# One kernel of four layers on Trainium2: the last score waves of the first attention in bank pairs, with one exponential for two heads

## The reference, cut to what matters

```python
h = layernorm(layernorm(x))                       # gamma, beta
q, k, v = heads(h @ w_qkv + b_qkv)                # 16 heads of 8 channels
scores = q @ k.T / sqrt(8)                        # 1024 x 1024 for each head
out = softmax(scores) @ v
x = x + x_in_norm + out @ w_out + b_out           # residuals
```

## Time and profile before

| | |
|---|---|
| median of 3 runs | 2932.99 us (2932.86 to 2940.77) |
| the profiled execution's own time | 2927.33 us |
| its span, first to last instruction | 2925.5 us |
| mean granted TensorE clock | 0.985 |
| first and last exponential of the first attention (L780) start | 68.1 and 860.1 us |
| busy in the span: PE, DVE, ACT, POOL | 94%, 79%, 72%, 62% |

### The profile page before, as it was taken

The page is one execution under the profiler, slowest core; times in us unless marked ns, Lnnn a source line. Parts: engine busy times, 40 slices in busy tenths (PEclk is TensorE's granted clock), DMA queues, the critical chain, the costliest instruction groups (busy, mean ns, idle before and its releaser), DMA issues.

```text
span 2925.5 us, 46589 instructions
## 1 busy us (share of the span) xinstructions
PE 2744.2 (94%) x16447; PEld 2037.2 (70%) x16447; DVE 2307.5 (79%) x4143; ACT 2100.6 (72%) x4692; POOL 1802.3 (62%) x1357
## 2 busy tenths in 40 slices
PE   6999999999899999999999999999999999999996
PEld 3333333333347777788888888888888888888885
DVE  8888888888937887778788777788777877777776
ACT  2777777777755555677777777777777777787773
POOL 3432534332115555677788778788778787777873
PEclk9999999999979999999999999999999999999997
DMA  1000000000021121000000000000000000000000
GB/s 41 7 7 7 12 7 7 7 7 2 2 76 53 47 73 59 8 1 1 1 1 3 1 3 3 3 1 3 3 1 3 3 1 3 3 1 3 3 3 6
DMA packets 25689, 34.83 MB, mean 12 GB/s; under 512 B 4136, under 2 KB 14952, under 8 KB 25456
## 3 DMA queue, kind: packets, MB, share of 16 engines
q1 hardware_dynamic: 25456, 31.85, 3.5%
HBM read 29.08 MB, written 2.23 MB: 11 GB/s over the span
## 4 chain that ended last, share of the span: by engine, by line
PE 69%; DVE 10%; ACT 10%; POOL 5%; issue 5%; DMA 0%; DVEq 0%; POOLq 0%
PE P L1792 17%; PE P L1817 11%; PE P L1660 9%; PE P L1645 5%; PE P L1721 5%; PE P L1803 5%; PE P L1633 4%; ACT a_PT L780 4%; PE P L1826 3%; PE P L1732 3%; PE P L1775 2%; PE P L1623 2%; DVE c_nm L1371 2%; ACT c_P L904 2%; POOL d_tn L1094 2%
## 5 line engine op out<-in xcount | busy, mean ns | idle before, releaser
L1371 DVE TENSOR_REDUCE c_nm<-P 128x1 f32<-128x1024 f32 x512 | 623.8, 1218 | 169.3 <-PE P L1792 169.1
L1216 DVE TENSOR_REDUCE a_mx<-P 128x1 f32<-128x512 f32 x1024 | 640.1, 683 | 94.9 <-PE P L1633 91.6
L904 ACT ACTIVATE c_P<-P,c_nm 128x1024 f32<-128x1024 f32 x512 | 576.0, 1125 | 131.6 <-DVE c_nm L1371 131.4
L780 ACT ACTIVATE a_PT<-P 128x512 f32<-128x512 f32 x1024 | 537.2, 602 | 165.5 <-PE P L1645 165.1
L2039 POOL TENSOR_TENSOR c_P<-c_P,c_P 128x1024 f32<-128x1024 f32 (+1 forms) x256 | 623.2, 2434 | 21.4
L2037 POOL TENSOR_SCALAR c_P<-c_P,c_rr 128x1024 f32<-128x1024 f32 (+1 forms) x256 | 304.4, 1189 | 305.0 <-DVE c_rr L1383 304.9
L1792 PE MATMUL P<-c_xth,c_Th 128*128 128x512 f32 x1024 | 365.8, 438 | 42.8 <-ACT c_P L904 42.6
L1645 PE MATMUL P<-a_Qs,a_Ks 32*128 32x512 f32 x1024 | 343.0, 491 | 59.1 <-ACT a_PT L780 52.6
L1817 PE MATMUL P<-c_DT,c_xkh 128*128 128x256 f32 x2048 | 392.0, 284 | 5.6 <-DVE c_xkl L1363 5.0
L1396 DVE TENSOR_TENSOR c_DT<-P,c_DT 128x512 fp32r<-128x512 f32 x512 | 348.6, 681 | 12.9 <-ACT c_DT L915 12.1
L1817 PEld LDWEIGHTS P<-c_DT,c_xkh 128*128 128x128 f32 x2048 | 330.1, 192 | 6.6 <-DVE c_xkl L1363 5.6
(11 more groups left out here) (245 smaller groups left out, 5418.4 us busy)
## 6 DMA issues: line engine op xcount, KB each, us to landing
b_cwB<-cw_scratch SPq DMA_DIRECT2D x64, 256.0 KB, 5.1
c_stg<-in_cw SPq DMA_DIRECT2D x8, 640.0 KB, 3.9
a_Qs<-a_mT SPq DMA_DIRECT2D x256, 2.0 KB
b_stg<-in_moe SPq DMA_DIRECT2D x9, 384.0 KB, 3.1
out<-xres SPq DMA_DIRECT2D x15, 128.0 KB, 1.8
xres<-in_x SPq DMA_DIRECT2D x3, 512.0 KB, 7.2
xres<-in_x SPq DMA_DIRECT2D x2, 256.0 KB, 3.1
a_hTl_f<-in_wqk SPq DMA_DIRECT2D x1, 512.0 KB, 3.7
```

Of the source, the lines that this page charges most:

```text
L780: e.activation(m.PT[j][hs % 4][:, :], bank("scores", u, hs, j), ACT.Exp, scale=SCALE).then_inc(m.S["a_exp"])
L904: e.activation(m.P1[s][n % 4][:, :], P[:, k:k + 2, :].rearrange("p c k -> p (c k)"), ACT.Exp, bias=m.nm[:, n % 4, s:s + 1], accum_out=m.sm ...
L1216: e.tensor_reduce(m.mx2[u % 2][:, t // 4, j, t % 4, half:half + 1], bank("maxima", u, t, j, half), AX, ALU.max).then_inc(m.S["a_max_dve"])
L1371: e.tensor_reduce(m.nm[:, n % 4, s:s + 1], P[:, k:k + 2, :].rearrange("p c k -> p (c k)"), AX, ALU.max, negate=True).then_inc(m.S["c_nm"])
```

## The change

For unit 15 and hs from 2 on, a step `pair` takes the place of two `scores` steps. Two heads (2 and 3, then 0 and 1) are multiplied into two neighbouring banks with one signal, and one exponential reads both, 1024 columns. The pairs alternate between banks (2, 3) and (5, 6). When the maxima have ended, `ring` shrinks to banks 0 and 1 and `act_ring` to bank 7. `a_PT` becomes one tensor, so that two heads' tiles are one operand; its size and order stay.

```diff
+SCORE_HEADS = ((2, 3), (0, 1))
+def paired(u, hs):
+    return u == NU - 1 and hs >= 16 - 2 * LAG0
+def scores_of(u, hs, j):
+    return ("pair", u, hs, 1 if j < 2 else 0) if paired(u, hs) else ("scores", u, hs, j)
...
+    score_pairs = Ring([(2, 3), (5, 6)])
...
+            if um == NU and m == 0 and i == 0:
+                ring.slots, ring.i, act_ring.slots, act_ring.i = [0, 1], 0, [7], 0
+            if 0 <= ue < NU and paired(ue, m_e):
+                if i % 2 == 0:
+                    p.on(score_pairs.take(), "pair", ue, m_e, i % 4 // 2)
+            elif 0 <= ue < NU:
                 p.on([act_ring.take()], "scores", ue, m_e, (i + 2) % 4)
...
-    m.PT = [[sb(f"a_PT{j}_{i}", [128, 512]) for i in range(4)] for j in range(4)]
+    m.PT = sb("a_PT", [128, 4, 4, 512])
...
 # ScalarE
+    def pair(u, hs, k):
+        first, j = v.plan.bank["pair", u, hs, k], SCORE_HEADS[k][0]
+        w.wait_ge(*at("a_st", "pair", u, hs, k))
+        w.wait_ge(*at("a_pv", "sums", *divmod(16 * u + hs - 4, 16)))
+        e.activation(m.PT[:, j:j + 2, hs % 4, :], P[:, first:first + 2, :], ACT.Exp, scale=SCALE).then_inc(m.S["a_exp"])
...
 # TensorE
+    def pair(u, hs, k):
+        c, kt = divmod(hs, 8)
+        bank("pair", u, hs, k)
+        first = v.plan.bank["pair", u, hs, k]
+        w.wait_ge(*at(f"a_mdma{u % 3}_{c}", "row2_low", u, c))
+        for i, j in enumerate(SCORE_HEADS[k]):
+            r = slice(32 * j, 32 * j + 32)
+            tt = e.matmul(P[:, first + i, :], m.Ks[u % 3][r, 128 * kt:128 * kt + 128],
+                          m.Qs[u % 3][r, 512 * c:512 * c + 512], start=True, stop=True)
+        tt.then_inc(m.S["a_st"])
...
-            w.wait_ge(*at("a_exp", "scores", u, hs, j))
+            w.wait_ge(*at("a_exp", *scores_of(u, hs, j)))
```

More of the change, by code:

```diff
@@ L169 @@
     "scores": {"a_st": 1, "a_exp": 1},
+    "pair": {"a_st": 1, "a_exp": 1},
     "sums": lambda u, hs: {"a_pv": 1, "a_oe": 1} if hs % 8 == 7 else {"a_pv": 1},
@@ L244 @@
     "scores": lambda *a: [("a_exp", "scores", *a)],
+    "pair": lambda *a: [("a_exp", "pair", *a)],
     "sums": lambda u, hs: [("a_oe", "sums", u, 15)],
@@ L362, in plan_all @@
                 on_ring("maxima", um, t, i % 4, half)
-            if 0 <= ue < NU:
+            if um == NU and m == 0 and i == 0:
[4 more added lines that the diff above has]
+            elif 0 <= ue < NU:
                 p.on([act_ring.take()], "scores", ue, m_e, (i + 2) % 4)
@@ L706, in a_free @@
 def a_free(v, *step):
-    return [v.at("a_oe", "sums", NU - 1, 7), v.at("a_oe", "sums", NU - 1, 15), v.at("a_st", "scores", NU - 1, 15, 1),
+    return [v.at("a_oe", "sums", NU - 1, 7), v.at("a_oe", "sums", NU - 1, 15), v.at("a_st", "pair", NU - 1, 15, 1),
             v.now("a_add", *step), v.now("a_rc", *step)]
@@ L779, in scores @@
             w.wait_ge(*at("a_pv", "sums", *divmod(16 * u + hs - 4, 16)))
-        e.activation(m.PT[j][hs % 4][:, :], bank("scores", u, hs, j), ACT.Exp, scale=SCALE).then_inc(m.S["a_exp"])
+        e.activation(m.PT[:, j, hs % 4, :], bank("scores", u, hs, j), ACT.Exp, scale=SCALE).then_inc(m.S["a_exp"])
+    def pair(u, hs, k):
[3 more added lines that the diff above has]
+        e.activation(m.PT[:, j:j + 2, hs % 4, :], P[:, first:first + 2, :], ACT.Exp, scale=SCALE).then_inc(m.S["a_exp"])
     def sums(u, hs):
@@ L1004, in l_gate @@
         tanh(bank("l_gate", i), i)
-    parts = dict(first=first, first_hn=first_hn, turn_h=turn_h, project=project, row2=row2, scores=scores, sums=sums,
+    parts = dict(first=first, first_hn=first_hn, turn_h=turn_h, project=project, row2=row2, scores=scores, pair=pair, sums=sums,
                  turn_o=turn_o, m_turn_x=m_turn_x, choose=choose, spread=spread, item=item, halves=halves, down=down,
@@ L1659, in sums @@
                 w.wait_ge(*at("a_oe", "sums", u - 1, 15))
-            tt = e.matmul(O[32 * j:32 * j + 32, :], m.Vp[b % 2][:, at_v:at_v + 32], m.PT[j][hs % 4][:, :],
+            tt = e.matmul(O[32 * j:32 * j + 32, :], m.Vp[b % 2][:, at_v:at_v + 32], m.PT[:, j, hs % 4, :],
                           start=(kt == 0), stop=(kt == 7))
@@ L1908, in l_down @@
         down_rows(ps[:, 0:128], i).then_inc(m.S["d_dn"])
-    parts = dict(turn_h=turn_h, values=values, project=project, maxima=maxima, row2=row2, scores=scores, sums=sums,
+    parts = dict(turn_h=turn_h, values=values, project=project, maxima=maxima, row2=row2, scores=scores, pair=pair, sums=sums,
                  divide=divide, turn_o=turn_o, out_project=out_project, m_turn_x=m_turn_x, route=route, spread=spread,
```

## The result

| | before | changed |
|---|---|---|
| median | 2930.15 us (2922.36 to 2940.77, 10 runs) | 2923.28 us (2916.74 to 2925.19, 10 runs) |
| ratio | | 0.9969, 95% interval 0.9955 to 0.9983 |
| profiled execution, span | 2925.5 us | 2921.5 us |

The change makes the kernel 0.31% faster, 9 us by the ratio (5 to 13 by its interval), where 13.5 were forecast. The time lies in the range, on the edge of what counts as a change.

What follows compares the result with a forecast made beforehand. Three banks for four heads were taken to stop TensorE once a wave. From 806.75 us, 37.5 us plus about 4 for low clock, with +0.65 at item 0, gave a 13.5 us gain on 2932.99: 2919.5 us, range 2909 to 2930.

Steps and rivals of the forecast that it cites:

- The bound: Waves after the last maxima: three banks for four heads stop TensorE once a wave, 0.63 us at clock 0.50.
- The wide exponential: ScalarE's 1024-column exponential: 1.03 us each, 0.92 us from one to the next; by pace alone 1.7 us saved.
- The wave: Four heads' scores, exponentials and sums: 1.96 us against 2.60 at clock 1.00, 2.64 against 4.06 at 0.50.
- the sum at 1.00: From the first pair at 806.75 to the end of the sums, all at full clock: 37.5 us.
- The first pair's wait: First pair needs banks 2 and 3, held by the last maxima until 806.71 us: +0.45 us.
- Item 0: First expert item, now on banks 0 and 1, waits for VectorE's divide and a signal: +0.65 us.
- The clock after: Changed kernel, first pair to end of sums: three stretches of 3.4 us at clock 0.50, costing about 4 us.
- The clock before: Old kernel after the last maxima: 34.1 us at clock 0.50, read from its profile.
- A clock as low as before: Rival for the same waves: 34.1 us at 0.50 remain, gain 6.4 us, 2926.6 us; chance 0.17.
- a costlier exponential: Rival: the 1024-column exponential costs 1.20 us, gain 10.6 us, 2922.4 us; chance 0.11.
- a gain given back: Rival: experts wait for `b_cwB` or a later stop absorbs the gain, 2933 us; chance 0.05.
- two pairs do not overlap: Rival: TensorE's next pair comes too late beside the exponential, waves of 3.1 us, 2940.7 us; chance 0.04.

Runs made afterwards that it cites:

- singles4: Like first56 with the same four score banks, but one 512-column exponential per head instead of one per pair; 2918.08 us, 0.9956 of the kernel before.
- one_pair: The changed kernel with one pair of score banks, (5, 6), in place of two; 2943.95 us, 1.0041 of the kernel before.
- first56: The changed kernel with the bank pairs in the order (5, 6), (2, 3) instead of (2, 3), (5, 6); 2915.86 us, 0.9946 of the kernel before.
- items23: first56 with the experts' bank pairs ordered (2, 3), (4, 5), (0, 1) instead of (0, 1), (2, 3), (4, 5); 2917.55 us, 0.9948 of the kernel before.
- route_third: first56 without two of the three passes of batch 0's two route steps; 2913.04 us, 0.9941 of the kernel before.
- stats_late: first56 with the next block's eight normalization statistics moved behind the last maximum, later steps shifted; 2915.46 us, 0.9945 of the kernel before.
- all4: stats_late with items23's order of experts' pairs and the third block's score pairs as (2, 3), (0, 1); 2912.84 us, 0.9938 of the kernel before.

## Why the prediction was right, and where it was off

- **The bound: right.** The stop for a bank once a wave was the loss; `singles4` and `one_pair` show it from both sides.
- **The wide exponential: right**, 1.02 and 0.92 us against 1.03 and 0.92.
- **The wave: right** at both clocks, 2.60 us at 0.50 against 2.64, and at 1.00, where no other step stands between two sums, 2.03 and 2.01 us against 1.96 (sums at 843.11 and 845.14, 847.58 and 849.59 in TensorE's timeline). My lower bound of 1.84 shows only within runs of four exponentials. From the first pair to the end of the sums it was 42.7 us, where I had 41.4 with 6.8 us less at 0.50; so the sum at 1.00 was somewhat too high. (Five groups of transposes, 0.66 + 4 x 0.55, are 2.9 and not 2.7, and the runs before spread over 7.9 and not 7.8 us; neither matters.)
- **The first pair's wait: the term that was mis-sized**, 2.66 us against 0.45. I took the scores at 806.37 for the first two heads of wave 2. By the order of the steps they are its last two: heads 2 and 3 stand before the sums of wave 0, and started by 804.9. The end of the maxima at 806.71 was read rightly; what is queued behind the waiting pair was not. The forecast is not off by this term: its sum starts at 806.75, 3.0 us after the `a_OT` copy, and the first pair did start 3.0 us after that copy. What it hid is what the order of the banks could still give.
- **Item 0: right**, 0.66 us against 0.65.
- **The clock after: too short**, 17.0 us at 0.50 against 10.2. The first fall lasted 10.2 us, over the stop of 2.66 and the slow waves behind it. With the pairs in the order of first56 it was 6.8 us (first56, singles4), 3.4 (items23) or absent (route_third), and with the statistics moved as well it was absent (stats_late, all4). The price was too low too: I had 0.9 us for 3.4 us at 0.50 in regular waves, and up to the routes items23 shows 1.6 for 3.4 and first56 2.6 for 6.8, both against route_third.
- **The clock before: a size taken from one execution.** My gain was against 34.1 us at 0.50. Three profiles have 34.1, 30.7 and 17.1, with stretches of 56.4 us on average, and 56.4 - 47.8 = 8.6 us is near what the timed runs show (9, from 5 to 13); three profiles 7 us apart allow no closer match than that. Against the profile that I had, the gain was 11.4. That is the larger part of 13.5 against 9. The rest, 2.1 us, is 1.2 from the first pair to the end of the sums, 0.3 from there to item 0, and the half microsecond that I added by leaning to one side. That the first of these is so small is partly luck: a clock that was low for longer, and dearer, met a sum at 1.00 that was too high.
- **Rivals.** A clock as low as before, a costlier exponential and a gain given back did not come. That two pairs do not overlap is the kernel one_pair, and it is slower, by 12 us where that rival had 7.7.

The Trainium skill ("TensorE: Matmul & The Clock Gate", A second HAM failure mode: psum-queue depth-cycling) has short stops between groups let the clock swing. The first two profiles of before agree (falls at 808.0 and 818.4 us in such waves), the third does not (none up to 827.3), and with the stops filled there was none in that place in the one profile taken. What decides in one execution stays open; I ran nothing that moves the stage in time and leaves all else.

## What to carry to other kernels

When an engine alternates with another over a ring of banks, count banks against the items of one round first: a missing bank costs a full stop each round, and a wider instruction gains little beside it, and loses where it takes the ring's last slack. When banks change hands between phases, list for each first user the last reader of its bank, and what is queued behind the waiter: in the stretch, turning the order of a ring was worth as much here as the wide exponential, two to three microseconds, though about half of it was the clock. A clock term read from one profile is a sample; profile the kernel before more than once before sizing a gain by it, and cut the stage at a common step: here one part repeated itself within 0.6 us and the other did not within 6. Compare the clock of two profiles before a difference of their times is put down to an edit.

## What the runs showed of the hardware that was not expected

- The kernel starts at clock 0.50 although TensorE is busy (63.66 of 71.7 us in the row above), and the clock rose for good at 79.4 to 95.7 us over 13 profiles, at about 81 in the first of before. The `a_OT` copy of unit 14 starts at 802.4 us where it rose at 79.4 (all4), and at 808.8 where it rose at 95.7 (items23): up to 6.5 us ahead of anything that was changed. The first profile of before shows 1.00 for this time, in the first slices of the earlier trace rows too, although its multiplications have the length that goes with 0.50; there the length tells the clock.
- Waves of 4.06 us at 0.50, with the steps between them, went on for 30.7 us in two profiles before the clock rose, and from the routes on for 17 to 19 us in all three. In all eight profiles of kernels with four score banks, whose waves are 2.60 us at 0.50, each stretch at 0.50 lasted 3.4 to 10.2 us, and from the routes on 6.8 at most.
